# Graph attention with layer norm: adjacency tiles pass through rows of the result, two turning places for tiles 0 to 8, values sorted by kind

## What is computed

```python
# x (2048, 256); adj (2048, 2048), 1 in 256 nonzero; Wq, Wk, Wv (256, 2048); Wout (2048, 256); h = 8
q, k, v = ((x @ W).reshape(8, n, 256) for W in (Wq, Wk, Wv))
a = einsum('hnd,hmd->hnm', q, k) / 16 + adj + adj
a = where(adj == 0, -1e6, a)
a = where(adj == 0, 0, softmax(a))
out = einsum('hnm,hmd->hnd', a, v).transpose(1, 0, 2).reshape(n, 8 * 256) @ Wout
return layernorm(x + out)
```

## Time and profile before

| | |
|---|---|
| runs | 1841.86, 1842.18, 1843.12 us, median 1842.18 |
| profiled execution | 1842.29 us; its span in the trace 1840.6 us |
| TensorE matmul busy | 1807.2 us, 98% of the span |
| VectorE, ScalarE, GpSimd busy | 61%, 46%, 54% |
| chain that ended last | TensorE on 86% of the span |
| granted TensorE clock, mean | 0.996 |

### The profile page before, as it was taken

One profiled execution on the slowest core, in us unless ns is written; L12 is line 12 of the kernel. 1 busy time (PEld: TensorE's weight loads), 2 busy tenths in 40 slices (PEclk: granted clock), 3 DMA queues, 4 the chain that ended last, 5 costly groups with the idle time before them and its releaser, 6 DMA issues.

```text
span 1840.6 us, 29367 instructions
## 1 busy us (share of the span) xinstructions
PE 1807.2 (98%) x10272; PEld 1580.4 (86%) x10272; DVE 1114.2 (61%) x2316; ACT 849.4 (46%) x1411; POOL 985.0 (54%) x764
## 2 busy tenths in 40 slices
PE   8999899999999999999999999999999999999997
PEld 7887789888898888988888888888888888898886
DVE  6898855556555565555555655556555555555666
ACT  5654544444544445444454435444454444453432
POOL 7888754444544456444564445544454444654443
PEclk9999999999999999999999999999999999999999
DMA  7888864666646666466664666556665566655664
GB/s 251 247 254 275 254 200 145 195 191 197 189 135 199 185 198 185 139 195 188 193 184 149 193 188 193 169 155 196 196 188 162 169 188 191 196 164 156 178 178 111
DMA packets 187027, 345.97 MB, mean 188 GB/s; under 512 B 39424, under 2 KB 96768, under 8 KB 170496
## 3 DMA queue, kind: packets, MB, share of 16 engines
q10 hardware_dynamic: 92224, 200.85, 34.8%
q1 hardware_dynamic: 94656, 143.24, 28.1%
HBM read 190.84 MB, written 18.87 MB: 114 GB/s over the span
## 4 chain that ended last, share of the span: by engine, by line
PE 86%; DVE 1%; SPq 0%; ACTq 0%; issue 0%; POOL 0%; DMA 0%; POOLq 0%; ACT 0%; DVEq 0%
PE bank L398 34%; PE y_bank L421 22%; PE bank L363 17%; PE y_bank L419 12%; PE y_bank L417 1%; SPq L302 0%; ACTq L567 0%; DVE blocks L654 0%; POOL p_split L472 0%; DMA p_turned<-blocks 0%; PE bank L383 0%; POOLq L254 0%; DVE y_acc L677 0%; DVE y_acc L674 0%; DVE ln L714 0%
## 5 line engine op out<-in xcount | busy, mean ns | idle before, releaser
L472 POOL TENSOR_TENSOR p_split<-p_turned,p_split 128x512 fp32r<-128x512 f32 x512 | 651.8, 1303 | 619.3 <-ACT p_split L539 619.1
L398 PE MATMUL bank<-k_split,q_split 128*128 128x512 f32 x3072 | 787.4, 392 | 0.0
L421 PE MATMUL y_bank<-v_split,p_split 128*128 128x512 f32 x1920 | 701.8, 399 | 0.0
L398 PEld LDWEIGHTS bank<-k_split,q_split 128*128 128x128 f32 x3072 | 576.2, 188 | 110.0
L631 DVE CUSTOM_DVE_ANT_0 t_p<-bank,m_sb 128x512 f32<-128x512 f32 x512 | 351.3, 687 | 365.7 <-PE bank L398 343.6
L419 PE MATMUL y_bank<-v_split,p_split 128*128 128x256 f32 x2048 | 555.8, 282 | 0.0
L530 ACT ACTIVATE t_p<-t_p,small 128x2048 f32<-128x2048 f32 x128 | 256.8, 2006 | 432.5 <-DVE small L643 423.5
L421 PEld LDWEIGHTS y_bank<-v_split,p_split 128*128 128x128 f32 x1920 | 362.6, 189 | 76.4
L419 PEld LDWEIGHTS y_bank<-v_split,p_split 128*128 128x128 f32 x2048 | 389.3, 190 | 18.3
L461 POOL TENSOR_TENSOR w_slot<-raw_w,w_slot 128x512 fp32r<-128x512 f32 x192 | 250.1, 1305 | 196.1 <-ACT w_slot L510 193.7
L654 DVE STREAM_TRANSPOSE blocks<-t_p 128x2048 f32<-128x2048 f32 x128 | 295.9, 2312 | 78.7 <-ACT t_p L530 66.7
(11 more groups left out here) (45 smaller groups left out, 712.7 us busy)
## 6 DMA issues: line engine op xcount, KB each, us to landing
m_sb<-m_dram ACTq DMA_DIRECT2D x112, 1024.0 KB, 5.2
p_turned<-blocks SPq DMA_DIRECT2D x1528, 64.0 KB, 2.1
p_turned<-blocks ACTq DMA_DIRECT2D x520, 64.0 KB, 2.6
blocks<-in_adj_dram SPq DMA_DIRECT2D x64, 256.0 KB, 3.9
raw_w<-in_L_gnn_Wv_dram ACTq DMA_DIRECT2D x64, 256.0 KB, 3.5
m_dram<-m_sb SPq DMA_DIRECT2D x16, 1024.0 KB, 6.4
raw_w<-in_L_gnn_Wq_dram ACTq DMA_DIRECT2D x63, 256.0 KB, 3.4
raw_w<-in_L_gnn_Wk_dram ACTq DMA_DIRECT2D x61, 256.0 KB, 3.9
```

The source lines that it names most:

```text
L398: mm = nc.tensor.matmul(dst[:], q[:, a, k, f * P:(f + 1) * P], k_split[:, kk, k, b * BANK:(b + 1) * BANK], start=(i == 0), stop=(i == len( ...
L421: mm = nc.tensor.matmul(y[:], hi, v_split[:, j].rearrange("p s d -> p (s d)"), start=False, stop=last)
L472: nc.gpsimd.tensor_tensor(lo, p_turned[:, i * BANK:(i + 1) * BANK].rearrange("p (j b) -> p j b", b=QUAD), hi.bitcast(F32), ALU.subtract).t ...
```

## The change

1. `adj_place(t, q)` becomes a function. Pieces q = 0 and 1 go through rows 12 to 15 of `y_acc` always, q = 2 and 3 through rows 8 to 11 up to tile 11 and through half of `blocks[1]` from tile 12 on. The loads of x into these rows of `y_acc` move behind the last use.
2. Tiles 0 to 8 and those from 14 on turn into two places in alternation, tiles 9 to 13 into `blocks[0]` alone. The turn of tile 14 waits for all mask pieces.
3. In the values, the four 512-column matmuls of a quarter come first, then its four of 256 columns. A quarter of the values stands ahead of the projections due in that quarter, and `LATER_V` is one quarter earlier, nearly throughout.
4. The end: ScalarE issues 4 instead of 8 of the shuffle DMAs of tile 126; the turn of tile 127 comes ahead of `add_y(124)`; two of the four low halves of tile 127 are made by VectorE; the root of part 0 is taken ahead of the last shuffle; the parts are tiles 0 to 11, 12 and 13, 14 and 15; stores are grouped anew.

```diff
-        adj_place = [blocks[1][:, i * BANK:(i + 1) * BANK] for i in range(BANKS)]
+        Y_FILLS = TILES - 4
+        ONE_PLACE, TWO_PLACES = Y_FILLS - 3, TILES - 2
+        def adj_place(t, q):
+            if q < 2 or t < Y_FILLS:
+                first = Y_FILLS + 2 * q if q < 2 else Y_FILLS - 4 + 2 * (q - 2)
+                return y_acc[:, first:first + 2, :].rearrange("p t d -> p (t d)")
+            return blocks[1][:, (q - 2) * BANK:(q - 1) * BANK]
...
         def turned_place(tau):
-            return blocks[0 if tau <= TILES else tau % 2]
+            return blocks[0 if ONE_PLACE <= tau < TWO_PLACES else tau % 2 if tau < ONE_PLACE else (tau + 1) % 2]
...
         def turned_before(tau):
-            return tau - 1 if tau <= TILES else tau - 2 if tau > TILES + 1 else None
+            if tau < ONE_PLACE:
+                return tau - 2 if tau >= 2 else None
+            if tau < TWO_PLACES:
+                return tau - 1
+            return tau - 2 if tau > TWO_PLACES else None
...
                    (2, 1): (("v", 5), ("vt", 7)), (2, 2): (("v", 6),), (2, 3): (("v", 7),)}
-        LATER_V = {(1, 3): (("vt", 0),), (2, 0): (("vt", 1),), (2, 1): (("v", 0), ("vt", 2), ("v", 1), ("vt", 3)),
-                   (2, 2): (("v", 2), ("vt", 4)), (2, 3): (("v", 3), ("vt", 5)), (3, 0): (("v", 4), ("vt", 6)),
-                   (3, 1): (("v", 5), ("vt", 7)), (3, 2): (("v", 6), ("v", 7))}
+        LATER_V = {(1, 2): (("vt", 0),), (1, 3): (("vt", 1),), (2, 0): (("v", 0), ("vt", 2), ("v", 1), ("vt", 3)),
+                   (2, 1): (("v", 2), ("vt", 4)), (2, 2): (("v", 3), ("vt", 5)), (2, 3): (("v", 4), ("vt", 6)),
+                   (3, 0): (("v", 5), ("vt", 7)), (3, 1): (("v", 6), ("v", 7))}
         FIRST_K = {(0, 0): (4, 5), (0, 1): (6, 7)}
...
         LAST_TILES = ALL - 2
-        EARLY_NORM = TILES - 3
-        NORM_PARTS = [slice(0, EARLY_NORM), slice(EARLY_NORM, TILES - 1), slice(TILES - 1, TILES)]
-        EARLY_OUT = EARLY_NORM // 2 * 2
+        ALL_M = TILES * BANKS
+        Y_LOADS = {1: (0,), 3: (1,), 5: (2,), 7: (3,), Y_FILLS - 1: (4, 5), TILES - 1: (6, 7)}
+        EARLY_NORM = TILES - 4
+        NORM_PARTS = [slice(0, EARLY_NORM), slice(EARLY_NORM, TILES - 2), slice(TILES - 2, TILES)]
+        FIRST_NORM = slice(0, 3)
...
-            return QUADS - 1 if tau < LAST_TILES else QUADS // 2
+            return QUADS - 1 if tau < ALL - 1 else QUADS // 2
...
                         m_of((t - 1) * BANKS + q)
-                    sp.dma_start(adj_place[q], adj_rows[t // 2, t % 2][:, q * BANK:(q + 1) * BANK]
+                    if t == Y_FILLS and q >= 2:
+                        for i in range(QUADS):
+                            sp.wait_ge(shuffled[i], 64 * (ONE_PLACE - 1))
+                    sp.dma_start(adj_place(t, q), adj_rows[t // 2, t % 2][:, q * BANK:(q + 1) * BANK]
                                  ).then_inc(adj_loaded[q], 16)
...
                         sp.wait_ge(y_loaded[c % 2], 16 * (c // 2))
+                    if c * HALVES >= Y_FILLS:
+                        m_of(ALL_M - BANKS + (c - Y_FILLS // HALVES))
+                    elif c * HALVES >= Y_FILLS - 4:
+                        m_of((Y_FILLS - 1) * BANKS + 2 + c - (Y_FILLS - 4) // HALVES)
                     sp.dma_start(y_acc[:, c * HALVES:(c + 1) * HALVES], x_pairs[c]).then_inc(y_loaded[c % 2], 16)
...
                         load_adj(t + 2, 0)
-                        if t % 2:
-                            load_y(t // 2)
+                        if t in Y_LOADS:
+                            for c in Y_LOADS[t]:
+                                load_y(c)
                     for i in range(QUADS):
...
-                sp.wait_ge(normed, 8)
-                store_out(0, 4)
                 sp.wait_ge(normed, EARLY_NORM)
-                store_out(4, EARLY_OUT // 2)
-                for t in range(EARLY_OUT, TILES):
+                store_out(0, EARLY_NORM // HALVES)
+                sp.wait_ge(normed, TILES - 2)
+                store_out(EARLY_NORM // HALVES, C - 1)
+                for t in range(TILES - 2, TILES):
                     sp.wait_ge(normed, t + 1)
                     sp.dma_start(out_tokens[t % 2][:, t // 2], y_tokens[:, t % 2, t // 2]).then_inc(stored, 16)
-                sp.wait_ge(stored, 16 * (2 * HALVES + TILES - EARLY_OUT))
+                sp.wait_ge(stored, 16 * 3 * HALVES)
...
                         wait_emptied(("v", h, 2 * g + 1))
-                    for j in range(TPB * g, TPB * (g + 1)):
-                        hi, lo = (p_split[tau % 2][:, part, j * P:(j + 1) * P] for part in (HI, LO))
-                        first, last = j == 0, j == CHUNKS - 1
-                        if first:
-                            nc.tensor.matmul(y[:], hi, v_split[:, j].rearrange("p s d -> p (s d)"),
-                                             start=True, stop=False)
-                        nc.tensor.matmul(y[:, 0:D], lo, v_split[:, j, HI], start=False, stop=False)
-                        if not first:
-                            mm = nc.tensor.matmul(y[:], hi, v_split[:, j].rearrange("p s d -> p (s d)"),
-                                                  start=False, stop=last)
+                    chunks = range(TPB * g, TPB * (g + 1))
+                    for j in chunks:
+                        nc.tensor.matmul(y[:], p_split[tau % 2][:, HI, j * P:(j + 1) * P],
+                                         v_split[:, j].rearrange("p s d -> p (s d)"), start=(j == 0), stop=False)
+                    for j in chunks:
+                        mm = nc.tensor.matmul(y[:, 0:D], p_split[tau % 2][:, LO, j * P:(j + 1) * P],
+                                              v_split[:, j, HI], start=False, stop=(j == CHUNKS - 1))
                     if g == BANKS - 1:
...
                             scores(tau, g)
+                        if LAG <= tau < LAST_TILES or tau >= ALL:
+                            values(tau - LAG, g)
                         for key in due(tau, g):
...
                                 project_x(key)
-                        if LAG <= tau < LAST_TILES or tau >= ALL:
-                            values(tau - LAG, g)
                     if LAST_TILES <= tau < ALL:
...
                     pool.wait_ge(m_scaled, by_pool[a])
-                    nc.gpsimd.tensor_tensor(m_piece(a), m_piece(a), adj_place[q].rearrange("p (r c) -> p c r", c=C),
+                    nc.gpsimd.tensor_tensor(m_piece(a), m_piece(a), adj_place(t, q).rearrange("p (r c) -> p c r", c=C),
                                             ALU.add).then_inc(m_by_pool, 1)
...
                             lo_p(tau - 2, 2 * b)
-                            lo_p(tau - 2, 2 * b + 1)
+                            if tau < ALL + 1:
+                                lo_p(tau - 2, 2 * b + 1)
                         if tau + 1 < TILES and b:
...
                                 hi_w(w_order[key] + 3)
+                        if tau == ALL and b == 1:
+                            sqrt_of(0, NORM_PARTS[0])
                         if 1 <= tau <= ALL and b == 2:
...
                             hi_wout(h)
-                    if tau == ALL:
-                        sqrt_of(0, NORM_PARTS[0])
                 sqrt_of(1, NORM_PARTS[1])
...
                 def turn(tau):
-                    if tau and turned_before(tau) is not None:
+                    if turned_before(tau) is not None:
                         for i in range(QUADS):
                             dve.wait_ge(shuffled[i], 64 * (turned_before(tau) + 1))
-                    elif tau:
+                    elif tau == TWO_PLACES:
                         dve.wait_ge(m_by_pool, len(by_pool))
...
                         dve.wait_ge(m_by_dve, by_dve[a] - 1)
-                    nc.vector.tensor_scalar(mark[:], adj_place[q], 0.0, None, ALU.is_equal, ALU.add,
+                    nc.vector.tensor_scalar(mark[:], adj_place(t, q), 0.0, None, ALU.is_equal, ALU.add,
                                             accum_out=chunk_count[:, q:q + 1]).then_inc(marked, 1)
...
                             out=m_piece(a), in0=mark[:].rearrange("p (r c) -> p c r", c=C), scalar=-BIG,
-                            in1=adj_place[q].rearrange("p (r c) -> p c r", c=C),
+                            in1=adj_place(t, q).rearrange("p (r c) -> p c r", c=C),
                             op0=ALU.mult, op1=ALU.add).then_inc(m_by_dve, 1)
...
+                def lo_p(tau, i):
+                    hi, lo = (by_chunk(p_split[tau % 2][:, part])[:, :, i, :] for part in (HI, LO))
+                    dve.wait_ge(p_hi, 4 * tau + i + 1)
+                    nc.vector.tensor_tensor(lo, p_turned[:, i * BANK:(i + 1) * BANK].rearrange(
+                        "p (j b) -> p j b", b=QUAD), hi.bitcast(F32), ALU.subtract).then_inc(p_lo, 1)
                 lo_of(("x", 0))
...
                     t = tau % TILES
+                    if tau == ALL:
+                        turn(tau - 1)
                     if tau > LAG:
...
```

(14 more changed lines are left out.)

## The result

The changed kernel takes 1827.38 us, the kernel before 1842.14 (medians of six runs each); the ratio is 0.9918, 95% interval 0.9906 to 0.9931. The forecast was 1825.5 us. The profiled execution of the changed kernel took 1826.67 us, its span is 1824.9.

A forecast was written before the change was run, and what follows sets the result against it. It took TensorE's matmul rate to bound most of heads 1 to 7, with waits only in late head 0 and the end. 10.9 + 2.4 + 3.5 = 16.8 us off 1842.3 gave 1825.5 us, range 1817 to 1836.5.

The forecast's parts named there:

- What bounds it: Most of heads 1 to 7: TensorE never idle, only matmul rate counts; it waits only in late head 0 and the end.
- Sorting: Value matmuls sorted by width: net 0.023 us a quarter over 476 quarters, 10.9 us off; bounds nothing to 25 us.
- Projections behind the values: Values ahead of projections, LATER_V a quarter earlier: same instructions, costed at nothing.
- The feared block at tile 2 of a head: Rival, 5%: early projections block TensorE on banks at tile 2 of seven heads, 50 us more, 1876 us.
- the one of indifferent widths: Rival, 13%: the order of matmul widths does not matter, only head 0 and the end gain, 1836.4 us.
- the rival in which the change-over cost goes too: Rival, 10%: scores behind narrow values also lose their change-over cost, sorting gives 25 us instead of 10.9, 1811 us.
- Head 0: Late head 0: tile 14's turn earlier gives 1.0 us, values ahead of k projections 1.4 us, together 2.4 us.
- The end: From tile 127's values on: low halves done earlier, VectorE then the bound, 3.5 us off; bounds 2.5 to 4.5.
- The last shuffle starts ... unchanged: At the end: despite four fewer ScalarE issues, the last shuffle still starts at about 1813.9 us.
- nine rows to normalise: At the end, behind VectorE's low halves: nine rows at 6.12 / 13 us each, 4.2 us.
- half clock for the last values would be hidden: At the end: TensorE at half clock in the last values would not lengthen the time, as VectorE is the bound.
- the later bound: At the end: VectorE's last low half waits out one of GpSimd's, ending at 1823.4; 0.6 us less gain.

The follow-up runs named there:

- e5: The changed kernel with a quarter's projections again ahead of its values and the old LATER_V, values still sorted: 1830.64 us, ratio 0.9949.
- e8: The changed kernel with values of two quarters taken together (eight wide, then eight narrow) in tiles 4 to 14 of heads 1 to 7: 1824.38 us, ratio 0.9916.
- e12: The changed kernel with whole-tile value runs (tiles 4 to 14 of heads 1 to 7; tiles 126, 127) and tile 127's low halves all on VectorE: 1822.67 us.
- e1: The changed kernel with the old alternation of wide and narrow value matmuls, all else as changed: 1835.96 us, ratio 0.9968.
- e2: The kernel before with the value matmuls sorted by kind within a quarter and nothing else: 1836.52 us, ratio 0.9971.
- e4: The kernel before with the new end alone: 1836.21 us, ratio 0.9971.
- e7: The changed kernel with all four low halves of tile 127 on VectorE, none on GpSimd: 1824.87 us, ratio 0.9916.
- e3: The kernel before with only the new adjacency places, turning places, x loads and waits of head 0: 1842.01 us, ratio 1.0002.
- e6: The changed kernel with the late x loads (tiles 11 and 15) issued ahead of the mask store and next adjacency load: 1826.31 us, ratio 0.9924.
- e9: The changed kernel with ScalarE again issuing 8 of the 16 shuffle DMAs of tile 126: 1828.39 us, ratio 0.9932.
- e10: The changed kernel with the turn of tile 127 again behind the addition of the values of tile 124: 1829.45 us, ratio 0.9931.
- e11: The changed kernel with all four low halves of tile 127 on GpSimd: 1828.66 us, ratio 0.9929.

## Why the prediction was right, point by point

The sum came nearer than its terms: 16.8 us forecast against 15.6 in the profiled pair (14.8 by the medians), with 4.0 too much for the sorting and 2.6 too little for the end. That these two cancel is luck.

**What bounds it** held: no idle TensorE from 300 to 1750 us in any of the fourteen kernels, and gains came from the rate and from the two places named. (VectorE was busy for 57% there, not half or less, which changes nothing.)

**Sorting**, right in its mechanism, off in size: 10.9 forecast, 6.9 measured, and in two shares, 4.5 from the sorting and 2.4 from the order of projections. The sum took every quarter as a plain one. It worked out 0.023 us a quarter from starts read to 0.01, where quarters without a projection gained 0.015 on average and those with one of 12 gained 0.007, and left out that a projection behind narrow values takes 1.44, not 1.43, and that in a quarter with a projection the change-over is paid twice or once depending on the order. The cost of a change that its own rows imply, 1.39 - 6 x 0.227 = 0.028 for the scores less 4 x 0.120 - 0.47 = 0.010 for the narrow ones, 18 ns, was right for longer runs: e5, e8 and e12 gave 18, 20 and 20.

**Projections behind the values** were costed at nothing in heads 1 to 7. This step failed: they gave 2.4 us there. The feared block at tile 2 of a head did not come; that rival is refuted by the busy times, the one of indifferent widths by e1 and e2. The formula that the prediction took for the second from the Trainium skill ("TensorE: Matmul & The Clock Gate", section "Back-to-back issue gap") is given there for a matmul on its own, not for a stream; no run here shows it, and in the streams here it is 0.227 us for 512 columns and 0.120 for 256. Of the rival in which the change-over cost goes too, nothing is left: scores take 1.39.

**Head 0**: 2.4 forecast, 2.6 in the profile after, but this agreement proves little. The turn of tile 14 came 2.0 us earlier with all edits and 1.2 with the turning places alone (1.0 forecast), and was not free at once, as foreseen. But the step had the wrong wait: not the adjacency add holds it last but ScalarE's exponential of the same tile, before (228.67) as after (227.08). So freeing the place was worth 0.4 us there, and the near hit on 1.0 is luck. What follows the turn depends on the clock. In the kernel with all low halves on GpSimd, whose head 0 is the same code, busy times and granted clock were:

```profile
206.60:210.00 3.40, 3.40 (x19) 2.86 (x18) 2.78 (x11) 0.68 (x2) 2.93 (x2) 1.00 0.67 169
220.40:223.80 3.40, 3.40 (x17) 3.17 (x16) 2.95 (x11) 1.69 (x3) 3.31 (x3) 0.56 0.59 161
230.50:237.30 6.80, 5.59 (x38) 5.21 (x39) 3.35 (x8) 1.95 (x4) 6.10 (x5) 1.00 1.06 334
```

It is at full clock from 230.5 to 237.3, where after had 0.52, and instead has a half-clock stretch at 220.4; it reaches tile 17 at 258.44, after at 260.85. Three kernels with the old head 0 (before, e2, e4) took 263.34 to 264.32, seven with the new one 258.44 to 262.28. So the new head 0 is faster by 1 to 6 us from one single execution to another. The medians say less. Take off from the gain in them what middle and end account for, and 14.8 - 13.0 = 1.8 us are left for head 0 in the changed kernel, 0.6 to 2.3 in e7 to e12. The same reckoning gives -1.0 and -1.2 for e2 and e4, which have the old turning places and order, so it is good to about 1 us. The gain of head 0 is then likelier 1 to 2 us than the 2.4 forecast, an estimate.

How much of this is the new turning places and how much the order of the values stays open. Alone, the places showed no gain (e3), and e5, which lacks the order, has -0.4 by this reckoning where e6 to e8 in its group have 0.7 to 2.3; this leans to the order, but does not show it. The late x load was not foreseen, and no cost of it shows (e6).

**The end**: 3.5 forecast, 6.1 measured. Three steps failed. "The last shuffle starts ... unchanged": it started 1.8 us earlier against the first score of tile 127, and e9 and e10 show that the shorter queue of ScalarE and the early turn are each worth something there (1.0 and 1.5 us). And nine rows to normalise were costed at the mean of before, 4.2 us; behind GpSimd they take 3.0. That mean held two rows of 1.3 us beside GpSimd. This also gave the low halves on VectorE their worth, 1.05 us by e11. The third is "half clock for the last values would be hidden". It did not come at all (waits of 0.61 us here and of 2.11 in e10 had full clock behind them, the one of 4.11 before had not), and it would not have been hidden: it made the last values 2.4 us longer before, and after VectorE adds them 0.2 us behind their end, so by these figures about 2 us would have shown, an estimate.

Where the 2.6 us between forecast and measurement lie, counted from the first score of tile 127: ScalarE's high halves end at 21.0 us where the sum had 22.9, but VectorE's low halves come 2.5 us behind them, not 1.4 and not even the 1.95 of the later bound, as VectorE is held in its rows beside GpSimd; they end at 23.5 instead of 24.3. Nine rows take 2.9 instead of 4.2, and all behind them 9.5 instead of 10.1: 0.8 + 1.3 + 0.5 = 2.6.

By edit, e9, e10 and e11 make 3.5 of the 6.1 us, if they add up. The 1.0 us of e2 is not to be added: e4, with the old order of values, had the full gain. The remaining 2.6 us (the root ahead of the shuffle, the parts of the normalising, and the half clock that went with the wait) were not taken apart.

## What to carry to other kernels

When the matmul engine is never idle, look at the order of widths: sum long runs of one width, compare with the mixed run, and count changes per loop body, neighbours included; but price a change from runs of the same length, as single matmuls in alternation pay less for each. Before moving work to hide a wait, ask which wait ends next: here the late x load, the freed turning places and the earlier turn of tile 14 moved waits of 1 to 2 us without moving the time by anything that the runs can tell. And give a small engine's last jobs to the faster one if the two hold each other up.

## What the runs showed of the hardware

- A change from narrow (256 columns) to wide (512) matmuls costs 18 to 20 ns net on TensorE between runs of four or more (e5, e8, e12). In alternation it costs less: 4 ns for each of 1098 (e2), 8 for each of 113 (e1). Scores behind narrow ones take 1.39 us for six, where 18 in the middle of a wide run take 0.227 each.
- Normalising a row (128x256, one source) takes VectorE 0.33 us alone. One that runs beside GpSimd's subtraction of a 128x512 piece takes up to 1.39, until 0.15 us after the end of that piece (before, after and e11 alike). The Trainium skill ("GPSIMD Engine Reference", section "8. Key points") names contention for VectorE's instructions with two SBUF inputs or in a 2-port perf mode; the two low halves on VectorE, which have two inputs, took 1.28 us behind GpSimd's, 3.03 beside them in e10, and four took 2.49 with GpSimd idle in e7.
- Head 0 of the same code differed by 3.8 us from one profiled execution to another, with half-clock stretches at different places. At the end, waits of 0.61 and 2.11 us had full clock behind them (after, e10), waits of 4.11 and 4.22 us half clock (before, e2).
